# FP4 levels in a feed-forward quantizer: rounding the bit pattern and two thresholds in place of seven thresholds

## The reference, cut to what matters

```python
_GRID = [0.0, 0.5, 1.0, 1.5, 2.0, 3.0, 4.0, 6.0]
_MID = [0.25, 0.75, 1.25, 1.75, 2.5, 3.5, 5.0]

def fp4_quant_dequant(x):                      # blocks of 16 along the last dim
    scale = jnp.max(jnp.abs(xb), axis=-1, keepdims=True) / 6.0
    scale = jnp.maximum(scale, 1e-12)
    xn = xb / scale
    idx = jnp.searchsorted(_MID, jnp.abs(xn))
    q = _GRID[idx] * jnp.sign(xn) * scale
...
gate = fp4_linear(x, w_gate)                   # fp4_linear rounds both of its inputs
y = fp4_linear(x, w_up)
return fp4_linear(silu(gate) * y, w_down)
```

## Time and profile before

| | |
|---|---|
| median of 3 runs | 5523.27 us (5519.79 to 5526.17) |
| the profiled execution's own time | 5521.02 us |
| its span, first to last instruction | 5519.3 us |
| the FP4 stage, its weight DMA to its last residual | 563.7 to 917.8 us of the span |
| busy in 604 to 918 us (314 us) | DVE 277.3, PE 168.6, ACT 74.8, POOL 45.6 us |

### The profile page before, as it was taken

One profiled execution on the slowest core, in us unless ns is written; L12 is line 12 of the kernel. 1 busy time (PEld: TensorE's weight loads), 2 busy tenths in 40 slices (PEclk: granted clock), 3 DMA queues, 4 the chain that ended last, 5 costly groups with the idle time before them and its releaser, 6 DMA issues. The chain is left out here.

```text
span 5519.3 us, 130512 instructions
## 1 busy us (share of the span) xinstructions
PE 4929.2 (89%) x50569; PEld 3352.3 (61%) x50569; DVE 3922.5 (71%) x6510; ACT 3359.4 (61%) x5923; POOL 2660.5 (48%) x1681
## 2 busy tenths in 40 slices
PE   6888555997899999999999999999999999799897
PEld 4444233554677667776777677766776777566544
DVE  5999797775677777777777677767777777477553
ACT  5776322554666666666666666666666666455444
POOL 4777110000566556665666566655555666266200
PEclk8999656998999999999999999999999999899898
DMA  2121000000000100010000000010001000000020
GB/s 84 61 77 62 4 0 7 2 1 19 17 12 12 29 14 11 11 30 15 11 11 20 25 11 11 12 30 12 11 11 33 12 11 11 14 2 2 24 62 19
DMA packets 76242, 113.90 MB, mean 21 GB/s; under 512 B 22496, under 2 KB 53424, under 8 KB 72048
## 3 DMA queue, kind: packets, MB, share of 16 engines
q1 hardware_dynamic: 67744, 110.60, 7.3%
q10 hardware_dynamic: 8256, 0.03, 0.1%
HBM read 70.38 MB, written 2.49 MB: 13 GB/s over the span
## 5 line engine op out<-in xcount | busy, mean ns | idle before, releaser
L2211 POOL TENSOR_TENSOR lt_qk<-lt_qk,lt_rot 128x1024 f32<-128x1024 f32 x384 | 907.0, 2362 | 207.3 <-DVE lt_rot L2575 207.3
L2221 POOL TENSOR_TENSOR lt_prob<-lt_prob,lt_total 128x1024 f32<-128x1024 f32 x192 | 365.1, 1902 | 1086.5 <-DVE lt_total L2597 1086.5
L2216 POOL TENSOR_TENSOR lt_qk<-lt_qk,lt_rnorm 128x1024 f32<-128x1024 f32 x384 | 726.2, 1901 | 110.5 <-ACT lt_rnorm L2451 102.9
L2258 PE MATMUL lt_ps<-lt_w_qk,lt_xs 128*128 128x512 f32 x1536 | 749.8, 611 | 23.0 <-DMA lt_scales<-in_L_scales 11.3
L2310 PE MATMUL lt_ps<-lt_z,lt_fold 128*128 128x256 f32 x3072 | 678.8, 379 | 1.3 <-ACT lt_z L2479 1.3
L2310 PEld LDWEIGHTS lt_ps<-lt_z,lt_fold 128*128 128x128 f32 x3072 | 583.6, 190 | 121.5 <-ACT lt_z L2479 24.4
L2572 DVE TENSOR_TENSOR lt_qk<-lt_ps,lt_table 128x1024 f32<-128x1024 f32 x384 | 467.8, 1218 | 79.0 <-ACT lt_sq L2441 72.1
L2575 DVE TENSOR_TENSOR lt_rot<-lt_ps,lt_table 128x512 f32<-128x512 f32 x768 | 490.1, 679 | 0.0
L2587 DVE TENSOR_REDUCE lt_nmax<-lt_ps 128x16 f32<-128x1024 f32 x192 | 229.9, 1197 | 360.5 <-PE lt_ps L2278 360.4
L2582 DVE TENSOR_REDUCE lt_norm<-lt_sq 128x16 f32<-128x1024 f32 x384 | 463.4, 1207 | 0.0
L2258 PEld LDWEIGHTS lt_ps<-lt_w_qk,lt_xs 128*128 128x128 f32 x1536 | 272.7, 193 | 253.9 <-issue 247.2
(11 more groups left out here) (406 smaller groups left out, 9935.5 us busy)
## 6 DMA issues: line engine op xcount, KB each, us to landing
mb_bs<-mb_rows SPq DMA_DIRECT2D x16, 1536.0 KB, 7.6
lt_xw<-lt_xw SPq DMA_DIRECT2D x192, 128.0 KB, 2.3
mb_bs<-mb_rows SPq DMA_DIRECT2D x16, 512.0 KB, 4.2
mo_gate_b<-mo_rows SPq DMA_DIRECT2D x16, 512.0 KB, 5.5
lt_xs<-h SPq DMA_DIRECT2D x96, 64.0 KB, 1.9
lt_w_qk<-in_L_ffn_Wqkv SPq DMA_DIRECT2D x6, 1024.0 KB, 4.9
lt_xs<-h SPq DMA_DIRECT2D x96, 63.8 KB, 1.9
lt_wvT<-in_L_wvT SPq DMA_DIRECT2D x6, 512.0 KB, 7.4
```

The source lines that it names most:

```text
L2211: pool.tensor_tensor(qk[:, u, :, :], qk[:, u, :, :], rot[:, u % 2, :, :], ALU.add).then_inc(sg["added"], 1)
L2216: pool.tensor_tensor(qk[:, u, :, :], qk[:, u, :, :], rnorm[:, u, :, :].to_broadcast([P, H, DH]), ALU.mult).then_inc(sg["qk"], 1)
L2258: last = pe.matmul(AT[u][:, 512 * k:512 * k + 512], xs[:, m.j, c:c + P], w_qk[:, a, 512 * k:512 * k + 512], start=True, stop=True)
```

## The change

It changes `Quantizer.dve` alone. The reciprocal is taken of `half`, not of `scale`, so the magnitude is twice as large as before, and that instruction now waits for `half`. The level is then found by keeping the exponent bits of the magnitude (a bitwise and on an int32 view), adding a quarter of that power of two less a little (a scalar_tensor_tensor), and cutting the mantissa to one bit (a second bitwise and), which rounds to the nearest of the larger levels. Two comparisons make a correction `low` for the small levels in a tile of its own, and a last instruction takes the larger of `level` and 2.0 and adds `low`. The eight full-width instructions were two tensor_scalar and six scalar_tensor_tensor; they are now three tensor_scalar and three scalar_tensor_tensor.

```diff
-    STEPS = 11
+    STEPS = 9
...
+        self.low = sb(name + "_low", [P, blocks, 16])
...
-        done(nc.vector.reciprocal(self.amax[:, :, :], self.scale[:, :, :]))
+        dve.wait_ge(sg[name + "_half"], n + 1)
+        done(nc.vector.reciprocal(self.amax[:, :, :], self.half[:, :, :]))
         dve.wait_ge(sg[name + "_mag"], n + 1)
         done(nc.vector.tensor_tensor(self.mag[:, :, :], self.mag[:, :, :], self.amax[:, :, :].to_broadcast(shape), ALU.mult))
         yield
-        dve.wait_ge(sg[name + "_half"], n + 1)
-        done(nc.vector.tensor_scalar(flat(self.level), flat(self.mag), 5.0, 2.0, ALU.is_gt, ALU.mult))
+        bits = flat(self.level).bitcast(I32)
+        done(nc.vector.tensor_scalar(bits, flat(self.mag).bitcast(I32), 0x7F800000, None, ALU.bitwise_and))
         yield
-        for mid in (3.5, 2.5):
-            done(nc.vector.scalar_tensor_tensor(out=flat(self.level), in0=flat(self.mag), scalar=mid, in1=flat(self.level),
-                                                op0=ALU.is_gt, op1=ALU.add))
-            yield
-        done(nc.vector.tensor_scalar(flat(self.level), flat(self.level), 2.0, None, ALU.mult))
+        done(nc.vector.scalar_tensor_tensor(out=flat(self.level), in0=flat(self.level), scalar=0.25 - 2.0 ** -23, in1=flat(self.mag),
+                                            op0=ALU.mult, op1=ALU.add))
         yield
-        for mid in (1.75, 1.25, 0.75):
-            done(nc.vector.scalar_tensor_tensor(out=flat(self.level), in0=flat(self.mag), scalar=mid, in1=flat(self.level),
-                                                op0=ALU.is_gt, op1=ALU.add))
-            yield
-        nc.vector.scalar_tensor_tensor(out=flat(self.level), in0=flat(self.mag), scalar=0.25, in1=flat(self.level),
-                                       op0=ALU.is_gt, op1=ALU.add).then_inc(sg[name + "_level"], 1)
+        done(nc.vector.tensor_scalar(bits, bits, 0x7FC00000, None, ALU.bitwise_and))
+        yield
+        done(nc.vector.tensor_scalar(flat(self.low), flat(self.mag), 1.5, -2.0, ALU.is_gt, ALU.add))
+        yield
+        done(nc.vector.scalar_tensor_tensor(out=flat(self.low), in0=flat(self.mag), scalar=0.5, in1=flat(self.low),
+                                            op0=ALU.is_gt, op1=ALU.add))
+        yield
+        nc.vector.scalar_tensor_tensor(out=flat(self.level), in0=flat(self.level), scalar=2.0, in1=flat(self.low),
+                                       op0=ALU.max, op1=ALU.add).then_inc(sg[name + "_level"], 1)
```

## The result

The changed kernel takes 5464.93 us (median of 4 runs, 5462.02 to 5472.71) where the kernel before took 5521.53 us beside it (4 runs, 5517.36 to 5526.17). The ratio is 0.9903, with a 95% interval of 0.9888 to 0.9918. The profiled execution alone would have lain inside the range.

What follows compares the result with a forecast made beforehand. VectorE bounds the `qh` halves; from product to residual addition the way over TensorE and ScalarE just covers it. Savings of 33.6 + 0.3 + 1.9 + 1.2 = 37.0 us gave 5484.0 to 5486.3, forecast 5485 us, range 5470 to 5500.

Steps and rivals of the forecast that it cites:

- the sum: Whole kernel: 33.6 + 0.3 + 1.9 + 1.2 = 37.0 us saved, so the profiled 5521.0 us become 5484.0.
- The halves of `qh`: VectorE's quantization of hidden values in 16 items: 2.10 us net saved per item, 33.6 us in all.
- the wait of 0.12 us: In each quantization the reciprocal must wait for `half`, starting 0.22 instead of 0.10 us behind it; 0.12 us counted as lost.
- The bitwise price: The new bitwise instructions on int32 cost what a tensor_scalar over the same tile costs, 0.56 us apart at 128x704.
- Rivals 2 and 3: Bitwise pass at two-tensor pace, 5499 us, chance 0.12; or as slow as dearest row, 1.95 us, 5538 us, chance 0.03.
- `qx`: Activation quantization: 0.93 us net per chain; items 1 to 14 give 0.3 us in all, items 0 and 1 give 1.9.
- Rival 1: The way over TensorE gets shorter too, L901 at the high clock, so all of `qx` is gained: 5472 us, chance 0.08.
- The start: Start of the FP4 stage, with shorter weight steps: item 0 starts 0.5 to 1.4 us earlier, taken as 1.2.
- the lower bound of 1.8: Start of the stage: VectorE waits for `fp_h_tok` over GpSimd, TensorE and ScalarE, 1.8 to 2.7 us.

Runs made afterwards that it cites:

- the kernel with 90 waits: The kernel before with 90 waits on a long-passed semaphore on VectorE behind the FP4 stage's last residual addition; 5513.41 us, ratio 1.0001.
- padded ones: The kernel before with 40 or 90 dead waits on VectorE behind the FP4 stage's last residual addition; 5508.74 us and 5513.41 us.
- with `qh` alone: The kernel before with the new quantizer steps for the hidden values only, the old ones for activations and weights; 5475.53 us, ratio 0.9926.
- the kernel with `qx` and `qw` alone: The kernel before with the new quantizer steps for activations and weights only, the old ones for the hidden values; 5506.35 us, ratio 0.9982.
- late_residual_before: The kernel before with item n-1's residual addition placed behind the second step of item n's `qh` quantization; 5511.86 us, ratio 0.9994.

## Why the prediction was wrong, and where it was right

**The step that failed** is the first paragraph's "The other stages do not use the changed code, so only these 314 us and the start of the stage can move." The local-transformer stage moved by 10.7 us, profile against profile. It moved as far when nothing was changed but dead waits ahead of it (3433.9, 3432.9 and 3432.4 us in the list as it was; 3423.7 and 3420.2 with waits added, one profile each). To that the sum is blind: it counts what the change executes, not where it puts the rest. With the 10.7 us and the 2.1 by which the FP4 stage beat the forecast, less 1.5 in other stages, the 5484.0 us of the sum become 5472.7, the profiled execution's own time. The last 8 us to the median of 5464.9 are a difference between single executions: nine runs of the changed kernel in two sessions go from 5462.0 to 5475.9, with a median of 5466.0, and both that were profiled (5472.7 and 5473.0) are among the slowest three. In which stage the faster ones gain is not shown. That the miss is a miss and not a hit hangs on these 8 us as much as on the 10.7: the profiled execution lies inside the range.

**How the place turns into 10 us stays open.** That VectorE's stalls move when the instruction list does is shown. But they don't add up to the time: the kernel with 90 waits has 11.5 us of them (5.4, 1.2, 1.6, 3.1, 0.2) and the shortest stage of the five profiles in which the arithmetic is that of before. What goes with the time better is TensorE's clock. Here is the end of the stage in windows of 10 us (as above; the third number from the end is the granted clock), in the second profile of the kernel before:

```profile
4755.90:4765.90 10.00, 5.07 (x14) 3.28 (x14) 1.78 (x4) 4.65 (x7) 0.00 (x0) 0.80 0.00 1
4765.90:4775.90 10.00, 2.90 (x6) 1.85 (x6) 6.90 (x17) 0.00 (x0) 0.00 (x0) 0.50 0.00 1
```

and in the changed kernel:

```profile
4710.30:4720.30 10.00, 6.87 (x29) 4.65 (x27) 1.26 (x3) 3.89 (x8) 0.00 (x0) 1.00 0.00 0
4720.30:4730.30 10.00, 1.53 (x6) 1.06 (x6) 8.17 (x20) 1.14 (x1) 0.00 (x0) 0.75 0.00 0
```

All three profiles at the old place end as the first, at 1.2 GHz with TensorE at its last matmuls; the last window of both padded ones is as the second (PE 1.5, DVE 8.2, clock 0.77 and 0.79). Summed over the stage from such windows of 8 us (twice one less the granted clock, times 8), TensorE is at 1.2 GHz for 85, 81 and 84 us in the three, for 74 and 63 in the two profiles of the changed kernel, and for 72 and 61 in the padded ones. Over 14 profiles the stage's time and this sum go together (correlation 0.87, 0.48 us of time for each us at the low level), so that the 15 us more at the low level in the three than in the two would answer to 7 of the 10. It does not hold for each: with `qh` alone TensorE is at the low level for 83 us, and the stage takes 3425.0. But a stall can make TensorE idle and so bring the clock down, and a clock that falls can make a stage long without a stall; no run here sets the one without the other.

**The halves of `qh`: mechanism right, size a little low.** Between the first reduction and the product of `qh` the 16 items took 167.0 us before and 131.6 after, 2.21 each and 35.4 together, where 33.6 was forecast. The mis-sized term is the wait of 0.12 us. It is there, 0.22 against 0.10, but costs nothing: the magnitude product cannot end earlier than 0.75 us behind GpSimd's, which starts with `half`. Before, `half` started at 900.70 and the product ended at 901.25 + 1.91 = 903.16, 2.46 us later; after, 703.35 to 705.81, 2.46 again. The rule of the Trainium skill that such a semaphore costs nothing extra, which I had set aside ("VectorE: DVE Perf Modes", The DRAIN you can't avoid), gives the right sum here; its reason, that the pipe is drained anyway, does not hold for this pair, since the reciprocal does start 0.12 us later.

**The bitwise price: right.** 587 and 527 ns at 128x704, as the two tensor_scalar of L741 and L747 had. Rivals 2 and 3 fall. With them goes the sentence that only L738 with its repeated operand is that slow: it was GpSimd's company.

**`qx`: right.** From product to residual addition the 16 intervals sum to 120.6 us before and 119.3 after: 1.3 us where 0.3 was allowed, and the rest of some 14 us is waiting, as the kernel with `qx` and `qw` alone shows from the other side. Items 0 and 1 gave 2.2 us (first reduction of `qx` to first product of `qh`, 29.69 to 25.28 us, less 2.2 for `qh`) where 1.9 was forecast.

**Rival 1: not seen.** `back` still starts behind an idle TensorE, the granted clock is 0.50, the 1.2 GHz level, over all of its L903, and that takes 2.93 us as before (714.91 to 717.84, in the item shown above); from product to residual addition it is 7.2 to 7.7 us in every item but the first, whose 7.33 became 6.83. Its time of 5472 us is near the result for another reason.

**The start: 0.2 us in this profile, 1.6 in the second, where 1.2 was forecast.** The last layer norm group ended at 603.40 in a stage that began 0.94 us later, so some 2.1 us later than before, not 0.9. The counted steps are right; what came on top are two idles of VectorE ahead of it, in the changed kernel:

```profile
589.57 0.69 DVE L287 TENSOR_TENSOR h<-cen,rstd 128x512 f32<-128x512 f32 x1 [0.91 <-ACT rstd L278]
592.32 0.75 DVE L748 TENSOR_SCALAR fp_qw_level<-fp_qw_level 128x1120 int32<-128x1120 int32 x1 [1.29 <-issue]
```

Before, there was one, a stall of 0.66 us. In the second profile of the changed kernel the first is absent and the second short:

```profile
589.76 0.74 DVE L748 TENSOR_SCALAR fp_qw_level<-fp_qw_level 128x1120 int32<-128x1120 int32 x1 [0.61 <-issue]
```

and item 0 starts 39.06 us behind the stage's first instruction, where it was 40.69 and, in the second profile of before, 40.71. The way over GpSimd, TensorE and ScalarE took 1.7 us in both, a little under the lower bound of 1.8, where VectorE's three instructions had taken 4.0. The term was sized rightly and came out at 0.2 by the chance of one execution; the kernel before has such executions too (a wait of 0.98 and a stall of 1.44 us in late_residual_before).

The FP4 stage adds up: 35.4 + 1.3 + 2.2 + 0.2 = 39.1 us, the measured difference, against 37.0 forecast. In the second pair of profiles it is 35.5 + 0.6 + 1.5 + 1.6 = 39.2 us.

## What to carry to other kernels

This long hand-ordered program has a part of its time that hangs on more than what it computes. A change that removes instructions moves all that follows, and here a stage without changed code was 10 us of 5500 shorter, a fifth of the whole gain and as large as the bound at which one can tell a gain at all. Before a gain or a loss of 0.2% is credited to an edit, compare the stages that it does not touch, give the kernel before a pad or two of dead waits to see how far it moves by itself, and take more than one profile of each, since one start of a stage differed by 1.5 us between two executions of the same program.

Where an edit turns work into waiting, the next edit is named by that wait: placing the residual addition one step later was worth 3.8 us before the change and 21.2 after it.

A row that is twice as slow as its like should be looked at beside the other engines' rows before its operand is blamed; then the wait that was priced at 1.9 us would have been priced at nothing.

## What the runs showed of the hardware

- A VectorE instruction with two tensors that meets a GpSimd product over 128x704 already under way takes 1.78 to 1.96 us instead of 0.89 and ends 0.75 us behind it, seen for two different instructions; one with one tensor keeps its 0.53. A GpSimd product of one block, 0.22 us long, leaves it nearly alone (0.92 us). Without the contention the FP4 stage took 295.0 us in one run, 19 to 20 less than the changed kernel's two profiles (313.9 and 315.0), 14.4 of it in the halves of `qh`; it can't be had by starting GpSimd a step later (315.6).
- A bitwise and on int32 over 128x704 takes 527 ns, like a tensor_scalar on f32.
- VectorE stalls of 0.2 to 5.9 us, waiting for nothing that the profile shows, stand at places of its program that recur every 128 instructions, at the first pass over the code. The long ones stand at the same place in two executions of one program (2.0, 4.5 and 2.0 us, then 1.9, 4.4 and 1.8), a short one may be absent, and the size can differ (1.29 and 0.61 us at one place).
